# A GNN kernel on one core: layer 0's own terms and head in three fp32r products, and the splits, tiles and window widths rearranged around them

## The chip, the core and the metric

The kernel runs on one core of a Trainium2 chip. The time is the device time of one execution in microseconds (us); lower is better. The engines are named as in the profile: PE is TensorE, DVE VectorE, ACT ScalarE, POOL GpSimd, SP SyncE. Each runs its own list of instructions in order; they meet only through semaphores.

## What is computed

625 nodes with 256 features, 10625 edges (`src`, `dst`, sorted by `dst`, self loops included), float32 throughout:

```python
def _edge_conv(x, src, dst, W, b):
    m = jnp.concatenate([x[dst], x[src] - x[dst]], axis=-1) @ W + b
    s = segment_sum(m, dst, 625);  cnt = segment_sum(ones, dst, 625)
    return s / jnp.maximum(cnt, 1.0)[:, None]

h = relu(layernorm(x)); xs = [h]
for W, b in ((W0, b0), (W1, b1), (W2, b2)):
    h = relu(_edge_conv(h, src, dst, W, b)); xs.append(h)
x = x + concatenate(xs, axis=-1) @ Wf + bf
h = relu(layernorm(x)) @ W                      # second block
agg = segment_sum(edge_weight[:, None] * h[src], dst, 625) + bias
out = x + relu(batchnorm(agg) * gamma + beta)
```

## The kernel before

**Reformulation.** With W split into its upper rows Wa (for `x[dst]`) and lower rows Wb (for `x[src]`), a layer is z / count + own: z is the count matrix (how often node s sends to node d) times u = h Wb, and own = h (Wa - Wb) + b, masked to nodes with an edge. The kernel builds the 625 x 625 count matrix, and a weighted one for the last block, once, then multiplies by it in each layer.

**Building the matrices.** Edges lie in 85 tiles of 125. For a tile `t`, `source_tile(t)` makes a one-hot of the sources (`src_hot`, 125 x 626, bf16): one DVE instruction, or two ACT instructions for the tiles in `SCALAR_TILES` (0, 4, 9, 36, 40, 55, 72, 76). The ring `src_hot` has 36 slots, so tile t waits until the tile 36 before it has been used. As the edges are sorted, the targets of a tile lie in a window of at most 28 nodes; `half_width(t)` gives the half of the range that is multiplied (6 to 14). `plain_window` and `weighted_window` make the target one-hots of 17 tiles at a time on DVE. PE multiplies, for each of five blocks of targets (r) and five of sources (s), all tiles that touch r (19 or 21 "pieces") into one bank of PSUM (L1215). In r = 0 it goes tile by tile; in r = 1 and 2 it goes through the first half of the pieces for all s, and then the second. ACT copies each finished block (`copy_block(r, s)`), and PE may start block (r + 1, s) only then.

**Interleaved with that.** PE's list goes: r = 0 with the transposes of h0 at the pieces named in `jobs` and the small vectors at piece 13; `neighbour_terms_0` (u of layer 0, fp32); r = 1; `own_terms_0` (fp32, eight products of 312 columns); r = 2; r = 3; r = 4; `sums_0` (z, in two halves of columns); `head_0` (h0 times the first 256 rows of Wf, fp32, ten products of 256 columns); then, for layers 1 and 2, `neighbour_terms`, `own_terms`, transposes of the weighted matrix, `sums`, `head`. The later layers don't multiply in fp32: an operand is split into a high part (ACT, a copy to fp32r) and a low part (DVE or POOL, operand minus high part), and `three` makes three fp32r products of them.

DVE's list is one loop over the 85 tiles, in which other work is put at fixed tiles: `U_AT` are the low parts of u in layer 0 (each waits for ACT's high part), `DIFF_AT` is Wa - Wb of layer 0, in place in `raw[0]`, `VECS_AT`, `DEV_AT` and `FLAG_AT` are small. After the loop follows a tail: `difference(1)`, `low_part(HI_WB1)`, `inverse_rows(0)`, `low_part(HI_WD1)`, `inverse_rows(1)`, `edge_rows_of(0)` and `(1)`, `difference(2)`; then the `z_step` and `h_low` of layer 0 and five `add_head(0, b)`, which release PSUM banks. POOL waits for `w_lo_vector` 1 (the tail's first low part), sums the weighted parts of r = 0 and 1, makes a low part, and masks the own terms of layer 0 (`mask_own_0`), for which the first `z_step` waits.

`Groups.plan` gives each group of products a bank of PSUM; `fill(name)` makes PE wait until the group that last used the bank has been read. For layer 1 the groups `("u", 1, b)` go to banks 5, 2, 3, 4, 6, and `("head", 0, b)` to banks 4, 6, 7, 0, 1: so `("u", 1, 3)` waits for `x1_added` 1, the first `add_head`, and `("u", 1, 4)` for the second.

## Time and profile before

| what | value |
|---|---|
| time, three runs | 121.03, 121.14, 122.48 us; median 121.14 |
| the profiled execution: its time | 121.92 us |
| the profiled execution: its span | 120.0 us (all times below count from its start) |
| granted TensorE clock, mean over the span | 0.978 of full speed |
| PE busy (matmuls) | 105.3 us, 88% |
| DVE busy | 96.7 us, 81% |
| ACT busy | 60.9 us, 51% |
| POOL busy | 27.3 us, 23% |
| DMA | 4.63 MB, nearly all of it before 12 us |

A row of a timeline gives the start, the busy time of the run of like instructions, the engine, the line, what is written and read with shapes, how many there are (x), and in brackets how long the engine had been idle and who released it. Durations of neighbours on an engine overlap a little, so a cost is best read from start to start.

### The profile page before, as it was taken

How to read it: one execution, taken by the hardware profiler on the slowest of the kernel's cores; microseconds unless marked ns; L12 is line 12 of the kernel's file. 1: busy time of each engine (PE TensorE's matmuls, PEld its weight loads, DVE VectorE, ACT ScalarE, POOL GpSimd, SP SyncE). 2: the span in 40 equal slices, each digit the busy share in tenths (PEclk: the TensorE clock that was granted, in tenths of full speed). 3: DMA queues.
4: the chain of work that ended last, by engine and by line, in shares of the span. 5: the costliest groups of instructions: out<-in, count | busy, mean ns of one | idle time of the engine just before them, and what ended most of it. 6: DMA issues, size and time to landing. Idle time of an engine off the chain costs nothing.

```text
span 120.0 us, 2668 instructions
## 1 busy us (share of the span) xinstructions
PE 105.3 (88%) x1023; PEld 97.5 (81%) x1023; DVE 96.7 (81%) x275; ACT 60.9 (51%) x143; POOL 27.3 (23%) x32
## 2 busy tenths in 40 slices
PE   0388999989999999999699999999899989999740
PEld 0236898968798999998599999999799979998540
DVE  2499995999999999989996579865999979527860
ACT  2596787986679999131560333331513154232530
POOL 7100000000000039964139910199000000000000
PEclk9999999999999999999999999999999999999965
DMA  1979500000020000500001100000000000000044
GB/s 45 227 194 267 182 2 5 0 5 0 3 87 5 0 5 5 177 8 0 0 0 45 48 0 0 0 5 0 0 0 5 0 0 0 3 0 5 0 102 112
DMA packets 5401, 4.63 MB, mean 39 GB/s; under 512 B 555, under 2 KB 5386, under 8 KB 5386
## 3 DMA queue, kind: packets, MB, share of 16 engines
q1 hardware_dynamic: 4460, 3.68, 10.9%
q10 hardware_dynamic: 926, 0.75, 2.4%
q8 instruction: 10, 0.16, 0.6%
q14 instruction: 5, 0.04, 0.1%
HBM read 3.79 MB, written 0.64 MB: 37 GB/s over the span
## 4 chain that ended last, share of the span: by engine, by line
PE 47%; DVE 38%; issue 6%; ACT 3%; DMA 2%; DVEq 0%; SPq 0%; ACTq 0%
DVE src_hot L567 14%; PE bank L1066 9%; PE bank L1068 9%; PE bank L1310 9%; PE bank L1067 9%; PE bank L1215 4%; DVE inv_count L643 3%; DMA edge_rows_i<-in_dst_dram 2%; DVE stats L517 2%; DVE raw L574 2%; PE bank L1350 2%; PE bank L1128 2%; DVE pre L729 2%; DVE pre L733 2%; DVE h_lo L739 1%
## 5 line engine op out<-in xcount | busy, mean ns | idle before, releaser
L1215 PE MATMUL bank<-dst_hot,src_hot 125*128 125x112 bf16 (+10 forms) x505 | 27.5, 213 | 1.6 <-DVE src_hot L567 1.0
L1215 PEld LDWEIGHTS bank<-dst_hot,src_hot 125*128 125x128 bf16 x505 | 25.1, 103 | 4.6 <-DVE src_hot L567 3.1
L567 DVE TENSOR_SCALAR src_hot<-node_id,edge_cols 125x626 bf16<-125x626 f16 x77 | 23.9, 377 | 0.0
L461 POOL TENSOR_TENSOR parts<-parts 125x625 f32<-125x625 f32 x5 | 7.0, 1394 | 48.7 <-DVE wb_lo L630 40.5
L1310 PE MATMUL bank<-counts,u_lo 125*128 125x312 f32 (+1 forms) x60 | 16.3, 308 | 0.0
L1010 ACT ACTIVATE h_hi<-pre 128x312 fp32r<-128x312 f32 (+1 forms) x12 | 5.6, 466 | 16.5 <-DVE pre L733 16.5
L1310 PE MATMUL bank<-counts,u_hi 125*128 125x312 f32 (+1 forms) x48 | 14.0, 307 | 0.0
L877 ACT ACTIVATE parts<-bank 125x375 f32<-125x375 f32 x25 | 12.9, 535 | 0.0
L1310 PEld LDWEIGHTS bank<-counts,u_lo 125*128 125x128 f32 x60 | 10.9, 189 | 0.0
L1310 PEld LDWEIGHTS bank<-counts,u_hi 125*128 125x128 f32 x48 | 9.1, 189 | 0.0
L877 ACT ACTIVATE counts<-bank 125x125 fp32r<-125x125 f32 (+1 forms) x25 | 7.9, 316 | 1.1 <-PE bank L1215 1.1
L1068 PE MATMUL bank<-wf_lo,h_hi 128*125 128x256 f32 x30 | 8.4, 281 | 0.0
L1066 PE MATMUL bank<-wf_hi,h_hi 128*125 128x256 f32 x30 | 8.4, 281 | 0.0
L1067 PE MATMUL bank<-wf_hi,h_lo 128*125 128x256 f32 x30 | 8.4, 281 | 0.0
L580 DVE TENSOR_TENSOR u_lo<-bank,u_hi 125x256 fp32r<-125x256 f32 (+1 forms) x13 | 5.7, 462 | 2.8 <-ACT u_hi L877 2.6
L877 ACT ACTIVATE u_hi<-bank 125x256 fp32r<-125x256 f32 (+1 forms) x13 | 5.3, 416 | 4.3 <-PE bank L1068 3.4
L877 ACT ACTIVATE weights_hi<-bank 125x500 fp32r<-125x500 f32 (+1 forms) x7 | 3.4, 546 | 7.6 <-PE bank L1350 7.6
L729 DVE TENSOR_TENSOR pre<-bank,inv_count 128x312 f32<-128x312 f32 (+1 forms) x12 | 5.7, 476 | 1.6 <-PE bank L1310 1.6
L733 DVE TENSOR_TENSOR pre<-pre,own 128x312 f32<-128x312 f32 (+1 forms) x12 | 6.3, 521 | 0.9 <-POOL own L472 0.5
L739 DVE SCALAR_TENSOR_TENSOR h_lo<-pre,h_hi 128x312 fp32r<-128x312 f32 (+1 forms) x12 | 6.3, 535 | 0.7
L1066 PE MATMUL bank<-weights_hi,u_hi 125*128 125x312 f32 (+1 forms) x20 | 6.2, 312 | 0.7 <-DVE u_lo L796 0.7
L905 ACT ACTIVATE distance<-node_id,edge_cols 125x626 f16<-125x626 f16 x8 | 6.6, 830 | 0.4 <-DVE edge_cols L551 0.2
(137 smaller groups left out, 260.4 us busy)
## 6 DMA issues: line engine op xcount, KB each, us to landing
raw<-in_L_gnn_W_dram SPq DMA_DIRECT2D x3, 512.0 KB, 6.7
x_in<-in_x_dram ACTq DMA_DIRECT2D x1, 560.0 KB
raw<-in_L_gnn_Wf_dram SPq DMA_DIRECT2D x1, 512.0 KB, 4.0
wf<-in_L_gnn_Wf_dram SPq DMA_DIRECT2D x1, 256.0 KB, 7.7
raw<-in_L_gnn_Wf_dram SPq DMA_DIRECT2D x1, 256.0 KB, 2.8
raw<-in_L_gnn_W_dram SPq DMA_DIRECT2D x1, 256.0 KB, 2.8
out_dram<-x_in SPq DMA_DIRECT2D x1, 224.0 KB
out_dram<-x_in SPq DMA_DIRECT2D x1, 168.0 KB
```

Of the source, the lines that this page charges most:

```text
L461: step.add(pool.tensor_tensor(part[:, :, 1, :], part[:, :, 1, :], part[:, :, 2, :], ALU.add))
L567: dve.tensor_scalar(src_hot[:, t % RING, 0:IDS], node_id[:, 0:IDS], edge_cols[:, 0, t:t + 1], None, ALU.is_equal).then_inc(src_hot_vector, 1)
L729: dve.tensor_tensor(pre_t[:, f, a:e], groups.bank[("z", l, q)][:, 0:e - a], inv_count[:, a:e], ALU.mult).then_inc(z_read, 1)
L733: dve.tensor_tensor(pre_t[:, f, a:e], pre_t[:, f, a:e], own[:, f, a:e], ALU.add).then_inc(z_ready, 1)
L739: dve.scalar_tensor_tensor(out=h_lo[l + 1][:, f, a:e], in0=pre_t[:, f, a:e], scalar=0.0, in1=h_hi[l + 1][:, f, a:e].bitcast(F32), op0=ALU.max,
L877: copy = lambda o, i: nc.scalar.activation(o, i, ACT.Copy)
L905: nc.scalar.activation(distance[:, :], node_id[:, 0:IDS], ACT.Abs, bias=edge_cols[:, 0, t:t + 1], scale=-1.0).then_inc(distance_ready, 1)
L1066: pe.matmul(o, lh, rh, start=start, stop=False)
L1067: pe.matmul(o, ll, rh, start=False, stop=False)
L1068: return pe.matmul(o, lh, rl, start=False, stop=stop)
L1215: return pe.matmul(built[s][:, :, n0:n0 + n], src_hot[:, t % RING, BLK * s:BLK * s + P], dst_hot[:, c, :, j // 2, c0:c0 + n, j % 2], start ...
L1310: ins = pe.matmul(bank[KF * h + f][:, 0:e - a], u[:, k, P * f:P * (f + 1)], counts[0:BLK, k, a:e], start=False, stop=(k == NB - 1 and u is ...
```

## The change

What it does, by place:

- `half_width` has two values, 10 and 14, where it had five (6 to 14). The number of pieces stays 101; the columns per block of sources go from 8256 to 8832.
- h0 is transposed at pieces 9, 11, 12, 14 and 15 (before: 12, 12, 14, 14, 16); ACT copies a transposed block after the next normalised one, not two later.
- Tile 36 goes from ACT to DVE.
- DVE's loop: `difference(0)` at tile 28 (before 37); the low parts of u at 34, 39 and 42 (27, 32, 35); new are the low part of Wa - Wb of layer 0 at 44 and the low parts of h0 at 46 and 48.
- ACT: new are three copies after r = 0 (the high part of Wa - Wb, two of h0) and one after r = 2 (the high part of Wf's first rows).
- `own_terms_0` and `head_0` use `three` on the split operands. `own_terms_0` waits for the new low parts.
- DVE's tail: the low part of Wf's first rows comes in, `low_part(HI_WD1)` and `difference(2)` go behind layer 0's last `h_low`, ahead of `add_head`. With that ACT's high part of layer 2's Wa - Wb goes behind layer 0's h, and `wf23_hi` into layer 1.
- POOL starts on `w_diff` 2, i.e. after `difference(1)`.

```diff
-SCALAR_EARLY, SCALAR_LATER = (0, 4, 9), {0: (36, 40), 1: (55,), 2: (72, 76)}
+SCALAR_EARLY, SCALAR_LATER = (0, 4, 9), {0: (40,), 1: (55,), 2: (72, 76)}
-STATS_AT, SHIFT_AT, VECS_AT, DIFF_AT = (1, 2, 3, 5, 6), 8, 19, 37
-U_AT = (27, 32, 35)
+STATS_AT, SHIFT_AT, VECS_AT, DIFF_AT = (1, 2, 3, 5, 6), 8, 19, 28
+WD0_AT, H0_AT = 44, (46, 48)
+U_AT = (34, 39, 42)
-    return min(WINDOW // 2, 2 * round(2.5 + 9 * math.sqrt(p * (1 - p))))
+    return 10 if 5 + 18 * math.sqrt(p * (1 - p)) < 10.75 else WINDOW // 2
+        h0_hi = sb("h0_hi", [P, KF, NODES_E], F32R)
+        (h0_lo,) = overlay(h0_base, arena_top[0], [("h0_lo", [P, KF, NODES_E], F32R)])
+        wd[0], (wf0_hi, wf0_lo) = wd[2], w4
-            pool.wait_ge(w_lo_vector, 1)
+            pool.wait_ge(w_diff, 2)
+                if t == WD0_AT:
+                    dve.wait_ge(layer0_hi, 1)
+                    dve.tensor_tensor(wd[0][1][:, :, :], raw[0][:, 0:KF, :], wd[0][0][:, :, :].bitcast(F32),
+                                      ALU.subtract).then_inc(layer0_lo, 1)
+                if t in H0_AT:
+                    f = H0_AT.index(t)
+                    dve.wait_ge(h0_hi_ready, f + 1)
+                    dve.tensor_tensor(h0_lo[:, f, :], h0_t[:, f, :], h0_hi[:, f, :].bitcast(F32),
+                                      ALU.subtract).then_inc(h0_lo_ready, 1)
             difference(1)
-            low_part(HI_WB1, wb[1][1][:, :, :], raw[1][:, KF:2 * KF, :], wb[1][0][:, :, :])
...
             inverse_rows(0)
-            low_part(HI_WD1, wd[1][1][:, :, :], raw[1][:, 0:KF, :], wd[1][0][:, :, :])
+            dve.wait_ge(layer0_hi, 2)
+            dve.tensor_tensor(wf0_lo[:, :, :], wf0[:, :, :], wf0_hi[:, :, :].bitcast(F32),
+                              ALU.subtract).then_inc(layer0_lo, 1)
+            low_part(HI_WB1, wb[1][1][:, :, :], raw[1][:, KF:2 * KF, :], wb[1][0][:, :, :])
...
-            difference(2)
...
                 h_low(l, 3)
+                if l == 0:
+                    low_part(HI_WD1, wd[1][1][:, :, :], raw[1][:, 0:KF, :], wd[1][0][:, :, :])
+                    difference(2)
                 if l < LAYERS - 1:
                     for b in range(NB):
                         add_head(l, b)
...
+                if r == 0:
+                    act.wait_ge(w_diff, 1)
+                    copy(wd[0][0][:, :, :], raw[0][:, 0:KF, :]).then_inc(layer0_hi, 1)
+                    for f in range(KF):
+                        copy(h0_hi[:, f, :], h0_t[:, f, :]).then_inc(h0_hi_ready, 1)
+                if r == 2:
+                    act.wait_ge(wf0_loaded, 16)
+                    copy(wf0_hi[:, :, :], wf0[:, :, :]).then_inc(layer0_hi, 1)
...
-                pe.wait_ge(w_diff, 1)
+                pe.wait_ge(layer0_lo, 1)
+                pe.wait_ge(h0_lo_ready, KF)
...
-                        ins = pe.matmul(o, raw[0][:, k, P * f:P * (f + 1)], h0_t[:, k, a:e],
-                                        start=(k == 0), stop=(k == KF - 1))
+                        ins = three(o, (wd[0][0][:, k, fc], wd[0][1][:, k, fc]), (h0_hi[:, k, a:e], h0_lo[:, k, a:e]),
+                                    k == 0, k == KF - 1)
...
-            jobs = {12: (0, 1), 14: (2, 3), 16: (4,)}
+            jobs = {9: (0,), 11: (1,), 12: (2,), 14: (3,), 15: (4,)}
```

## Rows read from the trace of the kernel before

**Rows 1.** Timeline of DVE, loop over tiles: start us, busy us, engine line op.

```profile
16.28 2.43 DVE L567 TENSOR_SCALAR src_hot<-node_id,edge_cols 125x626 bf16<-125x626 f16 x8
20.18 0.69 DVE L580 TENSOR_TENSOR u_lo<-bank,u_hi 125x512 fp32r<-125x512 f32 x1 [1.47 <-ACT u_hi L877]
...
29.91 0.41 DVE L556 TENSOR_TENSOR dst_hot<-pair_id,rel 125x504 bf16<-125x504 f16 x1
...
31.22 4.78 DVE L567 TENSOR_SCALAR src_hot<-node_id,edge_cols 125x626 bf16<-125x626 f16 x16
...
37.23 2.14 DVE L567 TENSOR_SCALAR src_hot<-node_id,edge_cols 125x626 bf16<-125x626 f16 x7
...
39.65 3.00 DVE L567 TENSOR_SCALAR src_hot<-node_id,edge_cols 125x626 bf16<-125x626 f16 x10
```

**Rows 2.** Timeline of PE: r = 1 to 4, own terms and head of layer 0.

```profile
21.81 3.57 PE L1215 MATMUL bank<-dst_hot,src_hot 125*128 125x4 bf16 x60
25.80 2.20 PE L1215 MATMUL bank<-dst_hot,src_hot 125*128 125x12 bf16 x45 [0.43 <-DVE src_hot L567]
27.86 4.46 PE L1139 MATMUL bank<-h_t,raw 128*128 128x312 f32 x16
32.16 2.40 PE L1215 MATMUL bank<-dst_hot,src_hot 125*128 125x12 bf16 x50
...
37.23 8.44 PE L1215 MATMUL bank<-dst_hot,src_hot 125*128 125x12 bf16 x181
...
52.70 4.48 PE L1149 MATMUL bank<-wf,h_t 128*125 128x256 f32 x20
```

**Rows 3.** Timeline of PE: neighbour terms, then own terms of layer 1.

```profile
59.87 0.38 PE L1066 MATMUL bank<-wb_hi,h_hi 128*125 128x256 f32 x1 [1.19 <-DVE h_lo L739]
...
60.67 0.28 PE L1066 MATMUL bank<-wb_hi,h_hi 128*125 128x256 f32 x1
...
62.10 0.31 PE L1066 MATMUL bank<-h_hi,wd_hi 128*128 128x312 f32 x1
...
65.59 1.03 PE L1350 MATMUL bank<-ident,parts 125*125 125x125 f32 x8
```

**Rows 4.** Timeline of ACT, after the copies of r = 2.

```profile
37.79 0.91 ACT L905 ACTIVATE distance<-node_id,edge_cols 125x626 f16<-125x626 f16 x1
...
41.03 0.61 ACT L877 ACTIVATE wb_hi<-raw 128x512 fp32r<-128x512 f32 x1
41.55 0.25 ACT L877 ACTIVATE counts<-bank 125x125 fp32r<-125x125 f32 x1
```

**Rows 5.** Timeline of DVE: the tail, and layer 0's first and last steps.

```profile
42.58 0.67 DVE L574 TENSOR_TENSOR raw<-raw 128x512 f32<-128x512 f32 x1
43.18 0.67 DVE L630 TENSOR_TENSOR wb_lo<-raw,wb_hi 128x512 fp32r<-128x512 f32 x1
...
45.84 1.32 DVE L630 TENSOR_TENSOR wd_lo<-raw,wd_hi 128x512 fp32r<-128x512 f32 x1
...
49.75 1.76 DVE L574 TENSOR_TENSOR raw<-raw 128x512 f32<-128x512 f32 x1
...
52.39 0.89 DVE L733 TENSOR_TENSOR pre<-pre,own 128x312 f32<-128x312 f32 x1 [0.49 <-POOL own L472]
...
59.73 0.41 DVE L656 TENSOR_TENSOR x_in<-x_in,bank 125x256 f32<-125x256 f32 x1
```

**Rows 6.** Timeline of POOL: first sum of weights, own terms masked.

```profile
43.93 1.30 POOL L461 TENSOR_TENSOR parts<-parts 125x625 f32<-125x625 f32 x1 [40.54 <-DVE wb_lo L630]
...
50.92 2.01 POOL L472 TENSOR_TENSOR own<-own,has_edge 128x312 f32<-128x312 f32 x2
```

**Rows 7.** Timeline of PE, the end of the kernel.

```profile
112.98 1.00 PE L1394 MATMUL bank<-ident,pre 128*125 128x128 f32 x5 [0.82 <-ACT pre L1052]
115.00 1.26 PE L1394 MATMUL bank<-ident,pre 128*125 128x128 f32 x4 [1.01 <-ACT pre L1052]
```

**Rows 8.** Busy time by stretch: start:end, length, PE busy, granted clock, DMA share, GB/s.

```profile
115.00:116.00 1.00, 1.00 (x4) 0.50 0.21 53
```

More of the change, by code:

```diff
@@ L223, in gnn_kernel @@
         shift = sb("shift", [P, NB], F32)
+        h0_base = arena_top[0]
         h0_t = sb("h0_t", [P, KF, NODES_E], F32)
@@ L316, in gnn_kernel @@
         h0_t_ready = sem("h0_t_ready")
+        h0_hi_ready = sem("h0_hi_ready")
+        h0_lo_ready = sem("h0_lo_ready")
+        layer0_hi = sem("layer0_hi")
+        layer0_lo = sem("layer0_lo")
         w_diff = sem("w_diff")
@@ L400, in gnn_kernel @@
                     (raw[2], rows(W4), raw_loaded[2], (w_lo_pool, 3))]
-        LO_W = (None, (w_lo_vector, 2), (w_lo_pool, 3))
+        LO_WB = (None, (w_lo_vector, 1), (w_lo_pool, 2))
+        LO_WD = (None, (w_lo_vector, 2), (w_lo_pool, 3))
         LO_WF1, LO_WF23, LO_W4 = [(w_lo_pool, n) for n in (1, 4, 5)]
@@ L942, in _ @@
                                      scale=rstd[0:BLK, b:b + 1]).then_inc(h0_ready, 1)
-                if b >= 2:
-                    h0_high(b - 2)
-            h0_high(3)
-            h0_high(4)
+                if b >= 1:
+                    h0_high(b - 1)
+            h0_high(NB - 1)
             def copy_block(r, s):
@@ L980, in _ @@
             high_part(wb[2][0][:, :, :], raw[2][:, KF:2 * KF, :])
-            act.wait_ge(w_diff, 3)
-            high_part(wd[2][0][:, :, :], raw[2][:, 0:KF, :])
             def turned(i):
@@ L1006, in _ @@
                         turned_high(i)
+                if l == 1:
+                    act.wait_ge(raw_loaded[1], 32)
+                    high_part(wf23_hi[:, :, :], raw[1][:, :, :])
                 for q, (f, h) in enumerate(QUADS):
@@ L1011, in _ @@
                 if l == 0:
-                    act.wait_ge(raw_loaded[1], 32)
-                    high_part(wf23_hi[:, :, :], raw[1][:, :, :])
+                    act.wait_ge(w_diff, 3)
+                    high_part(wd[2][0][:, :, :], raw[2][:, 0:KF, :])
                 if l == 1:
@@ L1137, in own_terms_0 @@
                     o = fill(("own", 0, q))[:, 0:e - a]
+                    fc = slice(P * f, P * (f + 1))
                     for k in range(KF):
-                        ins = pe.matmul(o, raw[0][:, k, P * f:P * (f + 1)], h0_t[:, k, a:e],
-                                        start=(k == 0), stop=(k == KF - 1))
+                        ins = three(o, (wd[0][0][:, k, fc], wd[0][1][:, k, fc]), (h0_hi[:, k, a:e], h0_lo[:, k, a:e]),
+                                    k == 0, k == KF - 1)
                     ins.then_inc(filled, 1)
             def head_0():
-                pe.wait_ge(wf0_loaded, 16)
+                pe.wait_ge(layer0_lo, 2)
                 for b in range(NB):
-                    o = fill(("head", 0, b))[0:BLK, 0:D]
-                    for k in range(KF):
-                        ins = pe.matmul(o, h0_t[:, k, BLK * b:BLK * (b + 1)], wf0[:, k, :],
-                                        start=(k == 0), stop=(k == KF - 1))
-                    ins.then_inc(filled, 1)
+                    project(("head", 0, b), feature_rows(h0_hi, h0_lo, b),
+                            [(wf0_hi[:, k, :], wf0_lo[:, k, :]) for k in range(KF)])
             def neighbour_terms(l):
@@ L1221, in _ @@
                     for i in range(len(pieces)):
+                        if i == 12:
+                            turn_vecs()
                         for b in jobs.get(i, ()):
                             turn_h0(b)
-                        if i == 13:
-                            turn_vecs()
                         wait_tile(seen)
@@ L1355, in _ @@
             for l in range(1, LAYERS):
-                pe.wait_ge(*LO_W[l])
+                pe.wait_ge(*LO_WB[l])
                 neighbour_terms(l)
+                pe.wait_ge(*LO_WD[l])
                 own_terms(l)
```

## The prediction

> **What bounds the kernel now.** I read the page's busy shares and chain first: PE and DVE are both busy most of the time, and the chain that ends last changes between them. So the question is which of the two ends last in each stage, and for that I went through the timelines of PE, DVE, ACT and POOL side by side.
>
> To 42.6 us the tiles of DVE lead. A tile costs 0.293 us (ten from 39.65 to 42.58), the two window instructions of 17 tiles 1.31 us (29.91 to 31.22). The loop has one real hole: tiles 19 to 26 begin at 16.28 and end at 16.28 + 8 x 0.293 = 18.62, and the next instruction, a low part of u, begins at 20.18 because ACT's high part is late [rows 1]. PE runs just behind: it waits for a tile at 25.80 in r = 1, does the own terms from 27.86 to 32.16 (4.3 us), r = 2 with two small jobs to 37.23 (5.07 us), r = 3 and 4 to 46.58, where it hardly waits [rows 2]. From 42.58 DVE's tail lasts to 51.9, and the first `z_step` then waits for POOL's mask until 52.39 [rows 5, 6]. DVE's steps of layer 0 lead on to 59.73, and PE, which had been idle for 1.19 us, goes on at 59.87. After that it is PE that leads through layers 1 and 2: the neighbour terms' last three blocks take 59.87 to 62.10, the own terms of layer 1 62.10 to 65.59, with no hole [rows 3]. So before 37 us what counts is when DVE's tiles and PE's r = 2 are done, from there to 59.8 POOL's start and DVE's steps, and after 59.87 each hole in PE.
>
> **The change, part by part.**
>
> *PE's own savings.* Own terms of layer 0: 4.30 us now [rows 2]. In three fp32r products they are the same 24 products as layer 1's, 3.49 us [rows 3]: 0.8 us less. Head: 52.70 to 57.04, 4.34 us; 30 products of 256 columns at the pace of 18 in 2.23 us (59.87 to 62.10) take 3.7 us: 0.6 us less. The head lies ahead of PE's 1.19 us of idle, which waits for DVE [rows 3], so its gain is worth nothing; the own terms' gain counts only if they can start in time.
>
> *DVE's loop up to tile 48.* Added are tile 36 (0.29), the low part of Wa - Wb (an operation like the one from 42.58 to 43.18, 0.60 us [rows 5]) and two low parts of h0. These have 626 columns instead of 512: 0.07 fixed and 0.53 x 626/512 make 0.72 each. Sum 2.33 us. `difference(0)` and the low parts of u only move. With the low parts of u at tile 34 and later, ACT's high parts (ready at 20.1) are long there, so the hole of 20.18 - 18.62 = 1.56 us goes. Net +0.8 us. The windows before tile 49 stood at 29.91 [rows 1] and come at 30.7; the second low part of h0 lies one tile ahead of them and is done at 30.4.
>
> *What waits for it.* `own_terms_0` now waits for both low parts of h0, i.e. until 30.45. When is PE there? Tile 35 comes at 18.62 + 8 tiles (2.34) + `difference(0)` 0.60 + windows 1.31 + low part 0.6 = 23.5 and is ready at 23.9, before PE's second half of r = 1, so the wait at 25.80 [rows 2] goes and r = 1 takes about 4.9 us from 21.8: ready at 26.7. Two widths and earlier transposes change r = 0 by at most 0.4 us either way (four of its 19 pieces go from 96 to 112 columns, and the last h0 transposes need `vecs`, which DVE makes at tile 19, as now); I take PE at 26.7 to 27.1. PE stands for 3.4 us or more, where it stood 0. The own terms run 30.45 to 33.95, and r = 2 begins 1.8 us later than at 32.16. Nothing can be put into this hole: r = 2 is behind the own terms in PE's list.
>
> *To the end of the tiles.* r = 2 ends at 33.95 + 5.07 = 39.0, its last block at 38.9. DVE reaches tile 68, which needs that block's slots, at 37.23 + 2 x 0.293 + 0.8 = 38.6 [rows 1], waits 0.3 and ends the tiles 1.1 us late, at 43.7. On ACT the copies of r = 2 end 1.8 us later than at 37.79; then there is a new copy of 512 columns (0.52, as from 41.03 to 41.55), tiles 72 and 76 (37.79 to 41.03, 3.24) and `wb_hi` 0.52. The first copy of r = 3 thus begins at 43.9 instead of 41.55 [rows 4], and PE's r = 4 waits for it until 44.45, where r = 3 ends at 44.1. Afterwards PE is 2.0 us late: z's first half, 46.58 to 49.5 now, is filled at 51.6.
>
> *The widths.* 576 more columns for each of 5 sources are 2880; at the pace of r = 2 that would be 1.2 us. But r = 3 and 4, with narrow pieces in them, take no less per piece (181 from 37.23 in 8.44 us, 47 ns with waits) than the first half of r = 2 (50 in 2.40 us, 48 ns with 112 columns [rows 2]). I take 0, the ends are -0.2 and +0.5.
>
> *Tail and POOL.* Out of the tail go a low part (1.3 us beside POOL) and `difference(2)` (1.7), in comes one low part of 0.6 to 1.3, and `wb_lo`, 0.6 now, may take 1.3 beside POOL [rows 5]. The tail of 8.9 us becomes 6.5 to 7.9, and DVE is ready for `z_step` at 51.6 at the latest. But it isn't DVE that opened it: POOL's mask did, seven us of work after its start at 43.93 [rows 6]. POOL now starts after `difference(1)`, one low part (0.6) sooner after the tiles: 43.93 + 1.1 - 0.6. So the first `z_step` is 0.5 us late, about 52.9, and z at 51.6 is just in time. Layer 0's steps keep their length: DVE is through with them at 60.3 instead of 59.73.
>
> *The moved work.* There now stand `low_part(HI_WD1)` and `difference(2)`, 0.60 each with POOL idle, ahead of the first `add_head` (0.41). PE starts its last three blocks of neighbour terms at 60.4, is ready for `("u", 1, 3)` 0.8 later (59.87 to 60.67 [rows 3]), at 61.2, and must wait for that `add_head`: 60.3 + 1.2 + 0.45 = 61.95. It was at 60.67: 1.3 us late in a stage where PE leads and had no hole. On ACT the high part for layer 2 waits for `difference(2)` until 61.5 and the high parts of u queue behind it; they are needed at 63 to 66, which leaves room. Wf's rows for the later heads are loaded from 61 instead of 47; needed past 67, so they are hidden.
>
> Sum at unchanged clock: +1.3 us (0.5 from POOL's start, 0.8 from the bank wait; the 1.8 to 2.0 us of PE are inside, absorbed but for that).
>
> *The clock.* PE would stand 3.4 us with nothing to do. The one fall of the clock in this trace comes after less: idle 0.82 us, five transposes, idle 1.01 us, and in 115 to 116 the granted clock is 0.50, the 1.2 GHz level [rows 7, 8]. An idle of 1.19 us did no harm: at 62.10 to 65.59 a product of 312 columns takes 0.145 us [rows 3]. 3.4 us is far beyond both, so the fall is likelier than not. A product of 312 columns takes 0.26 us at 1.2 GHz. The cost lies between 0 (no fall) and 24 x 0.115 = 2.8 us (all own terms low); I take nine products, 1.0 us, since it can fall only shortly before the 24 start and their dense work should bring it back. All of it arrives, because the sum above has used up PE's room.
>
> The Trainium skill speaks against the change here: "TensorE: Matmul & The Clock Gate", Part 1, has half clock as the state without work, released by activity, and its table at the end warns against idle gaps between bursts. By that rule the time is the one with 1.0 us in it, without it 1.0 us less.
>
> Total: +1.3 + 1.0 = +2.3. The sum is made in an execution with span 120.0 and time 121.92. Its start-to-start steps are the same in the others, so I put the difference on the median: 121.14 + 2.3 = **123.5**.
>
> **Rivals.**
>
> *The clock holds.* 121.14 + 1.3 = 122.5. For it: after the idle of 1.19 us nothing fell. Against: the hole is three times as long.
>
> *The delay is absorbed, no change.* PE and DVE lose at r = 2, but the tail is 2.3 us lighter. If POOL's path from 43.93 to 52.2 shrinks (its five operations of 1.30 alone are 6.5 of 7.0 us) by its 0.5 and DVE's low parts of h0 cost 0.6, layer 0 ends as now, and only the bank wait of 0.8 or less stays: 121.1 to 121.9, in the middle 121.5. Against: it needs each step to come out at its low end.
>
> *Faster.* The single mechanism is POOL's start: it follows the end of the tiles 0.6 us sooner, and POOL opens `z_step`. It decides if the low parts of h0 were ready when PE comes to them, so that the tiles end at 43.4 or sooner, and if PE's wait for the bank is hidden by the head's 0.6 us. That gives up to 0.6 + 0.5 less: 120.0. Against it: 30.4 against 26.7 to 27.1 is no close race.
>
> *The change's gain doesn't exist at all* (three products as slow as fp32): worth 0.8 us more in the own terms, 124.3; rows 3 show 3.49 us for that very shape, so I give it nothing of its own.
>
> **How the numbers follow.** Clock falls: 0.42, with 122.8 to 125.3 about 123.5, skewed upward, since the term's bound lies 1.8 above what I took. Clock holds: 0.33, 121.9 to 123.3. Absorbed: 0.15. Faster: 0.07. The rest, 0.03, is a clock that stays low into r = 2, above 125.3. The range of 8 in 10 leaves out the faster case with a little of the absorbed one, and the top: 121.2 to 125.0. A change by 2% is 2.4 us, about what can be told here: slower begins at 123.56. A little over half of the first case, a bit of the second and the rest are above: 0.36. Faster by over 2% (below 118.7) needs more than any mechanism above gives: 0.04. Within: 0.60.
>
> **What would show it.** Right: the second low part of h0 ends near 30.4 and PE's first own product is released by it, with 3 us or more of idle ahead; a granted clock below 1 between 27 and 36; tiles end near 43.7; the first mask of POOL opens `z_step` near 53; PE's eighteen products after layer 0 have a hole of about 0.7 us before `("u", 1, 3)`, released by `x_in`. Wrong: own terms that start at 27 to 28; tiles that end by 42.6; a `z_step` that starts near 51.5; or PE with no hole at 61.

## The result, and the profile after

| | before | after |
|---|---|---|
| time, us (median, lowest to highest) | 121.4 (121.03 to 122.48) | 124.92 (123.52 to 125.89) |
| ratio to before, 95% interval | 1 | 1.0237, [1.0172, 1.0301] |
| the profiled execution, us | 121.92 | 125.05 |
| its span, us | 120.0 | 123.2 |

The change costs 3.5 us by the medians, 2.9 us by the ratio, and 3.1 us by the two profiled executions, whose steps can be compared one by one. The ratio leaves out the slowest of after's four executions (125.89 us, mean granted clock 0.950), which counts as slow. The loss is clear of the noise; the interval does not decide whether it is more or less than 2%. I forecast 123.5 us in a range of 121.2 to 125.0: the time lies in the range, near its top, and what was forecast as 2.3 us is 2.9 to 3.5.

Busy shares and the clock's row on the page of after (busy us, share of the span, instructions; then the granted clock in 40 slices, 9 being 90% or more of 2.4 GHz):

```profile
span 123.2 us, 2705 instructions
...
PE 105.8 (86%) x1041; PEld 99.6 (81%) x1041; DVE 99.9 (81%) x274; ACT 62.1 (50%) x145; POOL 27.3 (22%) x32
...
PEclk9999999999589999999999999999999999999995
```

PE's clock is down in two places: near slice 10, which is new, and in the last slice, as before. The timeline of PE in after around the new one (start us, busy us, engine, line, operation, count, in brackets the idle time before it and what ended it):

```profile
23.00 4.92 PE L1245 MATMUL bank<-dst_hot,src_hot 125*128 125x12 bf16 x105
...
30.76 0.38 PE L1097 MATMUL bank<-h_hi,wd_hi 128*128 128x312 f32 x1 [2.84 <-issue]
30.98 0.31 PE L1098 MATMUL bank<-h_hi,wd_lo 128*128 128x312 f32 x1
...
32.01 0.46 PE L1097 MATMUL bank<-h_hi,wd_hi 128*128 128x312 f32 x1
...
34.95 0.31 PE L1097 MATMUL bank<-h_hi,wd_hi 128*128 128x314 f32 x1
...
35.82 2.41 PE L1245 MATMUL bank<-dst_hot,src_hot 125*128 125x12 bf16 x50
...
46.44 3.23 PE L1245 MATMUL bank<-dst_hot,src_hot 125*128 125x12 bf16 x76 [0.62 <-ACT parts L900]
```

And busy time by stretch of after (start:end, length, PE busy, granted clock, DMA share, GB/s):

```profile
30.00:31.00 1.00, 0.24 (x2) 1.00 0.00 0
31.00:32.00 1.00, 1.00 (x6) 0.65 0.00 0
32.00:33.00 1.00, 1.00 (x5) 0.50 0.00 0
...
34.00:35.00 1.00, 1.00 (x7) 0.64 0.00 0
35.00:36.00 1.00, 1.00 (x12) 1.00 0.00 0
```

Against [rows 2]: r = 1 has lost its wait for a tile and runs in one piece, but the own terms, which followed it without a gap at 27.86, begin at 30.76 after PE stood 2.84 us. The first products run at the high level; at 31.3 the clock falls to 1.2 GHz and is back at 34.7. The own terms take 5.06 us (30.76 to 35.82), longer than the 4.30 us of the fp32 products that they replace. The trace calls the releaser of the 2.84 us "issue"; the timeline of DVE shows whose end it matches, the second low part of h0, which runs from 29.86 to 30.66. The own terms begin 0.10 us behind it, and 0.09 to 0.11 us behind it in e1_fill, e2_early, e3_heads_first, e4_fp32_head, e7_combo and e11_moved_later too, wherever it lies.

```profile
29.86 0.80 DVE L629 TENSOR_TENSOR h_lo<-h_t,h_hi 128x626 fp32r<-128x626 f32 x1
...
40.88 1.56 DVE L577 TENSOR_SCALAR src_hot<-node_id,edge_cols 125x626 bf16<-125x626 f16 x5 [2.03 <-PE bank L1245]
...
45.64 0.67 DVE L584 TENSOR_TENSOR raw<-raw 128x512 f32<-128x512 f32 x1
...
48.31 1.33 DVE L683 TENSOR_TENSOR w_lo<-wf,w_hi 128x512 fp32r<-128x512 f32 x1
49.55 1.78 DVE L649 TENSOR_TENSOR wb_lo<-raw,wb_hi 128x512 fp32r<-128x512 f32 x1
...
53.33 0.67 DVE L667 TENSOR_SCALAR has_edge<-bank 128x250 f32<-128x250 f32 x2
53.92 0.47 DVE L749 TENSOR_TENSOR pre<-bank,inv_count 128x312 f32<-128x312 f32 x1
55.04 0.93 DVE L753 TENSOR_TENSOR pre<-pre,own 128x312 f32<-128x312 f32 x1 [0.65 <-POOL own L482]
```

DVE, which had passed the same place without a stop [rows 1], waits 2.03 us for r = 2's last block, and its tiles end at 45.64 instead of 42.58 [rows 5]. The two rows of POOL in after that answer to [rows 6]:

```profile
46.40 1.30 POOL L471 TENSOR_TENSOR parts<-parts 125x625 f32<-125x625 f32 x1 [42.99 <-ACT parts L900]
...
54.08 1.55 POOL L482 TENSOR_TENSOR own<-own,has_edge 128x312 f32<-128x312 f32 x2 [0.34 <-DVE has_edge L667]
```

The first row names ACT's copies as the releaser, but POOL starts 0.09 us after `difference(1)` has ended (45.64 + 0.67 = 46.31). It is 0.08 or 0.09 us in e4_fp32_head, e6_tail, e7_combo and e10_pool_start as well, so it is DVE that releases it, and the ACT copy that is named only ended at nearly the same time.

Last, PE in the neighbour terms of layer 1, against [rows 3]:

```profile
62.60 0.38 PE L1097 MATMUL bank<-wb_hi,h_hi 128*125 128x256 f32 x1 [0.54 <-DVE h_lo L759]
...
64.13 0.39 PE L1097 MATMUL bank<-wb_hi,h_hi 128*125 128x256 f32 x1 [0.57 <-DVE x_in L675]
```

Where the 3.1 us come from, by landmarks of the stages (us from the span's start, read off the timelines):

| landmark | before | after | difference |
|---|---|---|---|
| r = 0 done on PE, next stage begins | 17.41 | 18.61 | +1.20 |
| own terms of layer 0 begin | 27.86 | 30.76 | +2.90 |
| r = 2 begins | 32.16 | 35.82 | +3.66 |
| DVE's tiles end | 42.58 | 45.64 | +3.06 |
| first `z_step`: its addition | 52.39 | 55.04 | +2.65 |
| layer 0's last low part ends | 59.81 | 62.54 | +2.73 |
| own terms of layer 1 begin | 62.10 | 65.65 | +3.55 |
| the second output half's transposes | 115.00 | 118.51 | +3.51 |
| end of the span | 120.03 | 123.17 | +3.14 |

The loss is made by 35.82, 0.6 us of it is gone again by the end of the tiles, the tail gives 0.4 us back, and the moved work takes 0.8 us. From there the two run in step for 53 us. Before loses its clock at 114.81 and after at 120.05, which gives back 0.4 us at the end.

### The profile page after: what moved, and what is told of

It reads as the page before. It is cut to its first block, busy times and chain, and to the rows that moved or that the text cites. A ratio compares the mean times of both kernels' runs of the same rounds, so it can differ in the third digit from the quotient of the medians.

```text
span 123.2 us, 2705 instructions
## 1 busy us (share of the span) xinstructions
PE 105.8 (86%) x1041; PEld 99.6 (81%) x1041; DVE 99.9 (81%) x274; ACT 62.1 (50%) x145; POOL 27.3 (22%) x32
## 4 chain that ended last, share of the span: by engine, by line
PE 44%; DVE 28%; ACT 8%; issue 7%; POOL 7%; DMA 3%; SPq 0%; POOLq 0%; DVEq 0%; ACTq 0%
PE bank L1097 10%; PE bank L1099 10%; DVE src_hot L577 10%; PE bank L1098 10%; PE bank L1340 8%; DMA edge_rows_i<-in_dst_dram 3%; POOL parts L471 2%; POOL parts L473 2%; PE bank L1245 2%; DVE stats L527 2%; ACT parts L900 2%; PE bank L1380 2%; DVE pre L753 2%; DVE h_lo L759 1%; ACT distance L928 1%
## 5 line engine op out<-in xcount | busy, mean ns | idle before, releaser
L1245 PE MATMUL bank<-dst_hot,src_hot 125*128 125x112 bf16 (+6 forms) x505 | 27.6, 215 | 1.3 <-ACT parts L900 0.6
L1245 PEld LDWEIGHTS bank<-dst_hot,src_hot 125*128 125x128 bf16 x505 | 25.6, 104 | 3.8 <-DVE src_hot L577 1.8
L577 DVE TENSOR_SCALAR src_hot<-node_id,edge_cols 125x626 bf16<-125x626 f16 x78 | 24.7, 380 | 2.0 <-PE bank L1245 2.0
L471 POOL TENSOR_TENSOR parts<-parts 125x625 f32<-125x625 f32 x5 | 7.0, 1392 | 50.2 <-ACT parts L900 43.0
L1097 PE MATMUL bank<-h_hi,wd_hi 128*128 128x312 f32 (+1 forms) x24 | 8.2, 342 | 2.8 <-issue 2.8
L1098 PE MATMUL bank<-h_hi,wd_lo 128*128 128x312 f32 (+1 forms) x24 | 8.0, 335 | 0.0
L1099 PE MATMUL bank<-h_lo,wd_hi 128*128 128x312 f32 (+1 forms) x24 | 8.0, 333 | 0.0
L753 DVE TENSOR_TENSOR pre<-pre,own 128x312 f32<-128x312 f32 (+1 forms) x12 | 6.9, 573 | 1.0 <-POOL own L482 0.6
L1097 PEld LDWEIGHTS bank<-h_hi,wd_hi 128*128 128x128 f32 x24 | 5.1, 212 | 2.9 <-issue 2.9
L473 POOL TENSOR_TENSOR parts<-parts 125x625 f32<-125x625 f32 x5 | 6.8, 1369 | 0.4
```

What stands on the lines that cost most here:

```text
L471: step.add(pool.tensor_tensor(part[:, :, 1, :], part[:, :, 1, :], part[:, :, 2, :], ALU.add))
L473: pool.tensor_tensor(part[:, :, 0, :], part[:, :, 0, :], part[:, :, 1, :], ALU.add).then_inc(weights_summed, 1)
L577: dve.tensor_scalar(src_hot[:, t % RING, 0:IDS], node_id[:, 0:IDS], edge_cols[:, 0, t:t + 1], None, ALU.is_equal).then_inc(src_hot_vector, 1)
L753: dve.tensor_tensor(pre_t[:, f, a:e], pre_t[:, f, a:e], own[:, f, a:e], ALU.add).then_inc(z_ready, 1)
L1097: pe.matmul(o, lh, rh, start=start, stop=False)
L1098: pe.matmul(o, ll, rh, start=False, stop=False)
```

## The experiments

The four parts of the theory are: (1) the own terms wait for the low parts of h0, (2) this hole drops the clock, (3) the tail ends by POOL's and DVE's sums together, (4) the moved work opens a hole in layer 1. The rivals were that it is enough to fill the hole, that the cost sits in the head or in the widths, and that POOL's earlier start is a gain. All times are medians; "its own before" is the kernel before, run beside it on the same chip.

### e1_fill: the hole filled with products

```
                o = fill(("own", 0, 0))
                for _ in range(13):
                    pe.matmul(o[:, :], zeros_bf[:, :], node_id[:, 0:512], start=True, stop=True)
                pe.wait_ge(layer0_lo, 1)
```

The 13 added products write zeros into a bank that the own terms then start anew: they are extra work that changes no result.

> The changed kernel, with 13 products of zeros (512 columns, bf16) into the bank of the first own term, put on PE between r = 1 and the waits of own_terms_0; they fill 2.8 us of the hole and change no result. Theory (the clock costs 1.6 us, since the own terms took 5.06 us instead of 3.49): the own terms still start near 30.8 us, released by DVE, the granted clock stays 1.00 from 27 to 37 us, they take 3.5 us, and the whole is 1.3 to 1.6 us shorter than the changed kernel: 123.4 against 124.9. Rival (the clock is a bystander and the time is set by DVE, ACT and POOL after it): r = 2 begins 1.6 us sooner but the end moves by less than 0.4 us.

Measured: 123.65 us, 1.0139 [1.006, 1.0219] to its own before (121.93). PE in e1_fill:

```profile
27.49 2.97 PE L1167 MATMUL bank<-node_id,zeros_bf 125*128 125x512 f16 x13
...
31.12 0.39 PE L1097 MATMUL bank<-h_hi,wd_hi 128*128 128x312 f32 x1 [0.66 <-issue]
...
34.68 1.52 PE L1248 MATMUL bank<-dst_hot,src_hot 125*128 125x12 bf16 x30
```

and its stretches, in the same columns as above:

```profile
31.00:32.00 1.00, 0.88 (x6) 1.00 0.00 0
32.00:33.00 1.00, 1.00 (x9) 1.00 0.00 0
```

The own terms still wait, to 31.12, but they run at the high level and take 3.56 us instead of 5.06. r = 2 begins 1.14 us sooner than in after, the tiles end 1.14 us sooner (44.50), the span is 1.3 us shorter. By the ratios it is 1.2 us (1.0237 to 1.0139), but the two intervals overlap, so the times alone would not show it. The clock's fall is worth about 1.15 to 1.3 us, less than the 1.5 us by which the own terms got shorter, because they began 0.36 us later here.

That the fall comes from PE standing does not rest on this run alone. All four profiled executions with a hole of 2.7 to 3.0 us ahead of the own terms (after, e3_heads_first, e4_fp32_head, e11_moved_later) have a fall between 30.5 and 31.3 us and take 5.06 or 5.07 us for the own terms. All four in which the hole is filled, short or absent (e1_fill, e2_early, e9_early_fill, e7_combo) have none there and take 3.55 or 3.56 us. The profiled execution of e1_fill has another fall, from 13.53 to 16.94 us, ahead of the edit; r = 0 still ends 0.29 us sooner in it than in after.

### e2_early: the same low parts, up to seven tiles sooner

```
-WD0_AT, H0_AT = 44, (46, 48)
-U_AT = (34, 39, 42)
+WD0_AT, H0_AT = 38, (39, 40)
+U_AT = (34, 36, 37)
```

> The changed kernel, with the same splits at earlier tiles: low parts of u at 34, 36, 37, low part of Wa - Wb at 38, low parts of h0 at 39 and 40. DVE does the same work up to tile 48. Theory (PE's hole costs twice, as standing and through the clock): second low part of h0 done near 28.2 us instead of 30.7, hole of PE under 1 us, clock 1.00, r = 2 begins near 31.8 instead of 35.8; DVE then doesn't wait for r = 2 and its tiles end near 43.5 instead of 45.6; the whole is 2 us shorter, 122.9. Rival 1 (only the clock matters): 1.5 us shorter, as much as with the filling products. Rival 2 (DVE's added work sets the end of the tiles, not PE): tiles end near 45 and the gain is under 0.7 us.

Measured: 123.33 us, 1.0116 [1.0029, 1.0203], 1.6 us less than after by the medians where 2 were forecast. PE and DVE in e2_early:

```profile
28.15 0.39 PE L1097 MATMUL bank<-h_hi,wd_hi 128*128 128x312 f32 x1 [1.43 <-issue]
...
31.71 1.46 PE L1245 MATMUL bank<-dst_hot,src_hot 125*128 125x12 bf16 x29
...
43.40 0.67 DVE L584 TENSOR_TENSOR raw<-raw 128x512 f32<-128x512 f32 x1
```

The own terms now take 3.56 us without a fall of the clock, r = 2 begins 0.45 us ahead of before, and the tiles end 2.24 us sooner than in after. Layer 0 ends 2.26 us sooner (60.28). But the span is only 0.9 us shorter in this execution. Of that 2.26 us, 1.4 are lost again in layer 1, where two waits (times: us in total, how many, longest) and a fall of the clock stand:

```profile
PE bank L1097 <- DVE h_lo L759: 1.2, 1, 1.2
...
PE bank L1097 <- DVE x_in L675: 0.6, 1, 0.6
```

```profile
61.00:62.00 1.00, 0.44 (x4) 1.00 0.09 6
62.00:63.00 1.00, 1.00 (x7) 0.70 0.32 81
63.00:64.00 1.00, 1.00 (x7) 0.50 1.07 380
```

PE, sooner through z and the head, waits longer for layer 0, then again for `x_in`, and at 62.4 it falls to 1.2 GHz until 65.8. The other three executions have spans of 120.9, 120.7 and 121.9 us. So a hole mended in one place had moved to the next.

### e9_early_fill: e2_early with five zero products ahead of layer 1's third block

```
+                    if l == 1 and b == 2:
+                        o = fill(("u", l, b))
+                        for _ in range(5):
+                            pe.matmul(o[:, :], zeros_bf[:, :], node_id[:, 0:512], start=True, stop=True)
```

Here too the added products change no result.

> The kernel with the splits at earlier tiles (38, 39, 40), and in layer 1 five products of zeros ahead of the third block of neighbour terms, in the 1.2 us in which PE waits for DVE; they go into that block's own bank and change no result. Theory (in the run with the early splits the clock fell at 62.4 us, after holes of 1.18 and 0.56 us, and took 1.7 us back): the clock stays at 1.00 from 20 to 110 us, the end is 1.3 to 1.7 us earlier than with the early splits alone, near 121.0 of span or less. Rival (the fall there was chance, or the time isn't set by PE in layer 1): within 0.5 us of the run with early splits.

Measured: 123.30 us, 1.0119 [1.007, 1.0168], no faster than e2_early. In e9_early_fill's profiled execution the fall at 62.4 is gone, and the last output half begins at 116.27, 1.47 us sooner than in e2_early (117.74). The span is nevertheless 122.1, because SyncE's four issues of the last output transfers take 3.48 us, where they took 2.19 in e2_early:

```profile
59.01 1.25 PE L1189 MATMUL bank<-node_id,zeros_bf 125*128 125x512 f16 x5
...
116.10 3.48 SPq L437 DMA_DIRECT2D out_dram<-x_in  x4
```

One of the four took 1.87 us; the others take 0.37 to 0.49. The mean spans are 121.5 for e9_early_fill and 121.45 for e2_early. The forecast gain of 1.3 to 1.7 us did not come, and the rival named above it stands: the fall in e2_early may have been one execution's. A possible reading of the equal medians is that most executions of e2_early had no fall there. Neither that, nor that the products removed it in e9_early_fill, nor that it costs e2_early's median anything, is shown.

### e3_heads_first: the moved work behind the third `add_head`

```
-                if l == 0:
-                    low_part(HI_WD1, wd[1][1][:, :, :], raw[1][:, 0:KF, :], wd[1][0][:, :, :])
-                    difference(2)
                 if l < LAYERS - 1:
                     for b in range(NB):
+                        if l == 0 and b == 3:
+                            low_part(HI_WD1, wd[1][1][:, :, :], raw[1][:, 0:KF, :], wd[1][0][:, :, :])
+                            difference(2)
                         add_head(l, b)
```

> The changed kernel, with low_part(HI_WD1) and difference(2) behind the third add_head of layer 0 instead of ahead of the first. Theory (the moved work keeps PE waiting for a bank): the hole of 0.57 us before u of block 3 is gone, nothing else moves, 0.5 to 0.6 us shorter than the changed kernel. Rival (the wait is made up later, as DVE's work for layer 1 comes late anyway, or the moved work now makes own_terms of layer 1 or ACT's high parts late): less than 0.2 us, with a new hole between 63 and 68 us.

Measured: 125.48 us, with spans from 121.7 to 124.4: the times vary too much to say that it gained or lost. The trace says more. The wait of 0.57 us for `x_in` is gone: from layer 0's last low part (62.30) to layer 1's own terms (64.59) it takes 2.29 us, as before (59.81 to 62.10), against 3.11 in after. But `difference(2)` stands now ahead of the low parts of u, and PE waits for one of those. PE in e3_heads_first:

```profile
65.95 0.41 PE L1097 MATMUL bank<-h_hi,wd_hi 128*128 128x312 f32 x1 [0.33 <-DVE u_lo L590]
...
68.78 1.03 PE L1380 MATMUL bank<-ident,parts 125*125 125x125 f32 x8
```

The own terms of layer 1 take 4.19 us (64.59 to 68.78) instead of 3.49 [rows 3]: 0.8 us won, 0.7 lost. The wait was moved, not removed, as the rival had it.

### e11_moved_later: the two pieces apart

```
                         low_rows(("u", l, b), b, NB * l + b + 1)
+                    if l == 1:
+                        difference(2)
...
                     for b in range(NB):
+                        if l == 0 and b == 3:
+                            low_part(HI_WD1, wd[1][1][:, :, :], raw[1][:, 0:KF, :], wd[1][0][:, :, :])
                         add_head(l, b)
```

ACT's high part of layer 2's Wa - Wb, which needs `difference(2)`, goes into layer 1 with it.

> The changed kernel, with the low part of layer 1's Wa - Wb behind the third add_head and difference(2) behind the five low parts of u of layer 1 (the run that kept both together behind the third add_head got rid of one wait for a bank and got another, 0.33 us and slow products after it). Theory: with difference(2) out of the way the low parts of u come in time, PE has no hole from the third block on, own terms of layer 1 take 3.5 us and begin 0.8 us sooner after layer 0's last low part; spans 0.8 us shorter than the changed kernel's at a like clock. Rival (the stage is set by something else): no more than 0.2 us.

Measured: 123.73 us, 1.0107 [1.0031, 1.0182]. PE in e11_moved_later:

```profile
62.18 0.38 PE L1097 MATMUL bank<-wb_hi,h_hi 128*125 128x256 f32 x1 [0.55 <-DVE h_lo L759]
...
64.41 0.31 PE L1097 MATMUL bank<-h_hi,wd_hi 128*128 128x312 f32 x1
```

The stage is at 2.29 us again (62.12 to 64.41), and no new wait appears in the own terms behind it, which take 3.49 us (64.41 to 67.90). The gain is 1.2 us by the medians and 1.6 by the ratios, whose intervals just overlap. Only 0.8 of that is this stage by the traces. Another part is the start: r = 0 ends 0.30 us sooner in this execution than in after, the own terms of layer 0 begin 0.41 us sooner, and that lies ahead of the edit in the program, so the edit did not make it.

### e4_fp32_head: the head in fp32 again

```
-                pe.wait_ge(layer0_lo, 2)
+                pe.wait_ge(wf0_loaded, 16)
                 for b in range(NB):
-                    project(("head", 0, b), feature_rows(h0_hi, h0_lo, b),
-                            [(wf0_hi[:, k, :], wf0_lo[:, k, :]) for k in range(KF)])
+                    o = fill(("head", 0, b))[0:BLK, 0:D]
+                    for k in range(KF):
+                        ins = pe.matmul(o, h0_t[:, k, BLK * b:BLK * (b + 1)], wf0[:, k, :],
+                                        start=(k == 0), stop=(k == KF - 1))
+                    ins.then_inc(filled, 1)
```

With it go the high and the low part of Wf's first rows; the low part of h0 has memory of its own.

> The changed kernel, with the head of layer 0 in fp32 again: no high and low part of Wf's first rows (0.52 us on ACT after r = 2, 1.24 us in DVE's tail), low parts of h0 in memory of their own, since the head reads h0. Theory (the head's own gain lies in PE's idle, its splits lie on the path through ACT's tiles 72 and 76, and DVE's tail): head 0.7 us longer and unnoticed, r = 4 begins 0.5 us sooner, the first z_step 0.5 to 1.0 us sooner; the whole 0.5 to 1.0 us shorter. Rival (head's gain counts, the splits are hidden): up to 0.7 us longer.

Measured: 123.86 us, 1.0091 [1.0039, 1.0144] to its own before; 1.1 us less than after by the medians, 1.8 by the ratios, whose intervals do not overlap. DVE in e4_fp32_head:

```profile
48.01 1.32 DVE L648 TENSOR_TENSOR wb_lo<-raw,wb_hi 128x512 fp32r<-128x512 f32 x1
...
52.85 0.48 DVE L745 TENSOR_TENSOR pre<-bank,inv_count 128x312 f32<-128x312 f32 x1 [0.85 <-PE bank L1336]
...
54.05 0.93 DVE L749 TENSOR_TENSOR pre<-pre,own 128x312 f32<-128x312 f32 x1 [0.72 <-POOL own L481]
```

From the end of the tiles (45.34) to the first multiplication of `z_step` it is 7.5 us instead of 8.3, and there the block of z is what it waits for. The addition comes 8.7 us after the tiles instead of 9.4. PE's wait for ACT's copies ahead of r = 4 (0.62 us at 46.44 in after) is gone as well. Nothing later pays for the slower products. The three-product head is a loss by itself: it shortens PE where PE waits [rows 3] and lengthens DVE where DVE leads.

### e5_widths: before with the two widths

```
-    return min(WINDOW // 2, 2 * round(2.5 + 9 * math.sqrt(p * (1 - p))))
+    return 10 if 5 + 18 * math.sqrt(p * (1 - p)) < 10.75 else WINDOW // 2
```

> The kernel before with the two widths alone (half ranges of 10 and 14 instead of 6 to 14; 2880 more columns in all). Theory (pieces of 96 columns take 55 ns, those of 112 take 51, those of 64 as long as those of 80, so the width costs nothing on PE): r = 4 takes 4.0 us and the end of the span is within 0.3 us of before's. Rival (columns cost what the clock says, 0.42 ns each): r = 0 and r = 4 are 0.4 us longer each, the whole 0.4 to 0.8 us longer.

Measured: 122.02 us against 121.72, 1.0027 [0.9992, 1.0062]: no difference that can be told, and at most 0.75 us. PE in e5_widths, r = 3 and 4:

```profile
36.80 8.41 PE L1215 MATMUL bank<-dst_hot,src_hot 125*128 125x12 bf16 x181
```

The same 181 pieces took 8.44 us before [rows 2]: wider pieces at the edges cost nothing here.

### e10_pool_start: before with POOL's start alone moved

```
-            pool.wait_ge(w_lo_vector, 1)
+            pool.wait_ge(w_diff, 2)
```

> The kernel before, with POOL's start alone changed (after difference(1) instead of after the low part behind it). Theory of the prediction (POOL's mask opens the first z_step, and its start counts in full): z_step's add 0.6 us sooner, layer 0's last low part 0.6 us sooner, the whole 0.6 us shorter; the run with the lighter tail then owes the other 0.6 us of its 1.2 to fewer operations of DVE beside POOL's. Rival (DVE's tail is what opens it: the step can't start before the tail ends at 51.4 us with its add at 51.9): 0.5 us at z_step at most, and the whole at most 0.4 us shorter.

Measured: 121.29 us against 121.33, 0.999 [0.9953, 1.0028]. POOL, then DVE in e10_pool_start:

```profile
43.64 1.69 POOL L461 TENSOR_TENSOR parts<-parts 125x625 f32<-125x625 f32 x1 [40.24 <-ACT parts L877]
```

```profile
52.52 0.83 DVE L733 TENSOR_TENSOR pre<-pre,own 128x312 f32<-128x312 f32 x1 [0.53 <-POOL own L472]
```

POOL starts 0.76 us behind the end of the tiles instead of 1.35 (43.93 - 42.58 [rows 5, 6]), but its first sum now runs beside `wb_lo` and takes 1.69 instead of 1.30. The addition comes 9.64 us after the tiles instead of 9.81. Of 0.6 us, 0.17 arrive there, and nothing that can be told at the end.

### e6_tail: before with a lighter tail

On the kernel before, own terms and head in fp32: POOL's start as in e10_pool_start, and `low_part(HI_WD1)` and `difference(2)` out of the tail, to the places that they have in e11_moved_later:

```
-            low_part(HI_WD1, wd[1][1][:, :, :], raw[1][:, 0:KF, :], wd[1][0][:, :, :])
             inverse_rows(1)
...
             edge_rows_of(1)
-            difference(2)
...
+                    if l == 1:
+                        difference(2)
...
+                        if l == 0 and b == 3:
+                            low_part(HI_WD1, wd[1][1][:, :, :], raw[1][:, 0:KF, :], wd[1][0][:, :, :])
                         add_head(l, b)
```

ACT's high parts for layer 2 and for Wf move with them, and PE waits for the low part of layer 1's Wa - Wb only ahead of the own terms, no longer ahead of the neighbour terms.

> The kernel before, with only its DVE tail and POOL's start changed, and layer 0 left in fp32: POOL starts after difference(1), the low part of layer 1's Wa - Wb goes behind the third add_head, difference(2) behind the five low parts of u of layer 1. Theory (the tail and POOL's start open the first z_step, and the moved work is harmless where PE doesn't wait for it): tiles end as before near 42.6, the first z_step's add starts near 51.8 instead of 52.4, no hole at the third block's bank, and the end is 0.6 us earlier than before. Rival (it only moves the wait: POOL's operations collide with DVE's and take longer, or the low part of Wa - Wb comes late for PE): within 0.2 us of before.

Measured: 120.35 us against 121.72, 0.9888 [0.9854, 0.9922]: faster than both kernels, and by 1.4 us where 0.6 were forecast. DVE, then POOL in e6_tail:

```profile
42.46 0.67 DVE L575 TENSOR_TENSOR raw<-raw 128x512 f32<-128x512 f32 x1
...
49.40 0.48 DVE L728 TENSOR_TENSOR pre<-bank,inv_count 128x312 f32<-128x312 f32 x1 [0.83 <-PE bank L1313]
...
51.08 0.94 DVE L732 TENSOR_TENSOR pre<-pre,own 128x312 f32<-128x312 f32 x1 [1.20 <-POOL own L473]
```

```profile
43.22 1.68 POOL L462 TENSOR_TENSOR parts<-parts 125x625 f32<-125x625 f32 x1 [39.81 <-ACT parts L880]
...
46.24 1.30 POOL L462 TENSOR_TENSOR parts<-parts 125x625 f32<-125x625 f32 x1
...
50.12 1.55 POOL L473 TENSOR_TENSOR own<-own,has_edge 128x312 f32<-128x312 f32 x2
```

POOL's third sum in before, for comparison:

```profile
46.57 1.76 POOL L461 TENSOR_TENSOR parts<-parts 125x625 f32<-125x625 f32 x1
```

The addition comes 8.62 us after the tiles instead of 9.81: 1.2 us, of which POOL's start has 0.17 (e10_pool_start). The rest is that DVE no longer runs `wd_lo` and a difference beside POOL: the third sum takes 1.30 us instead of 1.76, the two masks 1.55 instead of 2.01, 0.92 of the 1.0 us. The 1.3 us stay to the end: the own terms of layer 1 start at 60.83 instead of 62.10.

### e7_combo: all mends on the kernel after

The edits of e9_early_fill, e11_moved_later and e4_fp32_head together.

> All mends together: splits at tiles 38, 39, 40; head of layer 0 in fp32 without its splits; low part of layer 1's Wa - Wb behind the third add_head and difference(2) behind the low parts of u of layer 1; five products of zeros in the hole of layer 1. Theory: what is left of the change is own terms in three products, 0.8 us more of DVE work before the tiles end, POOL's earlier start and a lighter tail. Tiles end near 43.4, first z_step's add near 52.0, no fall of the clock before 110 us; span 119.5 to 120.2, i.e. as before or 0.4 us less. Rival (own terms in three products are worth their splits): over 1 us less than before.

Measured: 122.04 us against 121.72, 1.0033 [1.0008, 1.0059]. PE in e7_combo:

```profile
28.20 0.38 PE L1090 MATMUL bank<-h_hi,wd_hi 128*128 128x312 f32 x1 [0.36 <-issue]
```

r = 2 begins at 31.75, 0.4 us ahead of before, and still DVE's tiles end at 43.45 instead of 42.58, for the low parts of Wa - Wb and h0, and tile 36, are on DVE. The first addition is at 52.13 where e6_tail has it at 51.08. So the own terms in three products buy nothing even when they hardly wait. The 1.7 us between e6_tail and e7_combo are not theirs alone, though: widths, transposes, tile 36 and the zero products differ too.

## Why the prediction was right, and where it was off

- **The own terms wait for the low parts of h0.** Right: forecast to end near 30.4, measured 30.66; forecast idle 3.4 us or more, measured 2.84. The hole was shorter since r = 0 ended 1.2 us later, which I had put at 0.4 us at most: the trace's record of the clock begins with a rise at 17.65 instead of 15.83 (the views show 1.00 before it, but two transposes take 0.63 us at 16.77 and 0.39 at 17.66), so that more pieces of 112 columns and transposes ran at the low level. It did no harm, as PE had to wait anyway. This was chance, not the change: e2_early and e9_early_fill have the same instructions up to layer 1, and their first rise is at 14.61 and 18.07, the end of r = 0 at 17.41 and 18.74.
- **The clock falls.** Right, and the term was mis-sized: 1.0 us by nine slow products, measured 1.57 (5.06 - 3.49), by 13 products in 3.4 us. The step "it can fall only shortly before the 24 start" failed: it fell after the hole, 0.5 us into the own terms. e1_fill gives 1.15 to 1.3 us of it back at the end. By the Trainium skill, "TensorE: Matmul & The Clock Gate", Part 1, half clock is what PE has without work; the trace agrees that a hole brings it, but it came when PE was at work again.
- **The tiles.** DVE's wait for r = 2's block was forecast at 0.3 us, 1.3 with the clock, and is 2.03; the tiles end at 45.64, forecast 43.7 and 44.7 with the clock. The missing 0.9 us are the 0.6 of the clock and 0.3 by which the own terms began later. z's first half, forecast filled at 51.6 or 52.6 with the clock, has its last product start at 53.66; DVE took it at 53.92 without a recorded wait, so this added nothing. PE's wait for ACT's copies ahead of r = 4, forecast 0.35, is 0.62 at 46.44.
- **The tail.** Mis-sized: 6.5 to 7.9 us forecast, 8.3 measured (45.64 to 53.92). The one low part "of 0.6 to 1.3" is 1.24, and `wb_lo` is 1.71, for which I had allowed 1.3. Both run beside POOL.
- **POOL opens `z_step`.** Half right. The row at 55.04 has POOL as its releaser, as forecast, and the addition is 0.4 us sooner after the tiles than before, where I had 0.6. But POOL had itself waited 0.34 us for DVE's `has_edge`. e10_pool_start shows the step "one low part (0.6) sooner" to be wrong as a gain: POOL's start alone gives 0.17. What gives time is the work taken away from beside POOL (e6_tail). In after `wb_lo` and the new low part took its place.
- **The bank wait in layer 1.** Right: forecast about 0.7 us of hole released by `x_in`, measured 0.57 at 64.13, and the stage is 0.82 us longer. e11_moved_later removes it, 3.11 to 2.29 us.
- **Widths at 0, head's gain at 0.** Right (e5_widths, within its interval; e4_fp32_head). Of the head I had only seen that it gains nothing; that its splits cost 0.7 us at the first addition, and about 1 us or more in all, I had inside the tail and not named.
- **The sum.** 0.5 + 0.8 + 1.0 = 2.3 forecast. By the traces, at the same places: 2.65 at the first addition (forecast 1.5 with the clock), 0.8 to 0.9 in layer 1 and -0.4 at the end, 3.1. The miss of 0.8 us by the traces (0.6 to 1.2 by the times) comes from ahead of the first addition: clock 0.6, start of the own terms 0.3, tail 0.2, less the 0.4 at the end. So the mechanisms were as forecast and the term of the clock was the one sized worst.
- **The rivals.** The clock did not hold; e1_fill, which keeps it up, comes to 1.0139, near that rival's 122.5 over 121.14, a ratio of 1.011. The delay was not absorbed. The faster case needed the low parts of h0 by 26.7 to 27.1; in e2_early, which comes nearest at 28.1, the layer still ends 0.5 us later than before.

What stays open: how often e2_early loses its clock in layer 1 (one profiled execution shows it), and where the rest of the difference between after and e11_moved_later comes from. The price of the clock also differs between executions of after: their mean clocks of 0.973, 0.984, 0.977 and 0.950 make 6.5, 3.9, 5.7 and 12.4 us at the low level (twice the missing share of the span), and only the first was profiled. The move of tile 36 and the earlier transposes were not tried alone. Whether the own terms would pay with the low parts of h0 made by ACT or POOL was not tried.

## What to carry to other kernels

Before products are made cheaper by splitting their operands, ask which engine makes the parts and when: here 0.8 us on PE were bought with 2.0 us of low parts on DVE (0.60 + 2 x 0.72), which led, and the parts came 2.8 us after the products could have run. A hole in a busy PE is priced twice, as the wait and as the clock behind it, so the work that precedes it must be ready first or the split not made. Where two engines both use the same memory, look for operations to take out of the overlap before moving a start: the start gave 0.17 us, the lighter overlap 1.0.

## What the runs showed of the hardware

- The clock fell at 31.3 us, 0.5 us after a hole of 2.84 us had ended, and was back at 34.7. Holes of 2.95, 3.03 and 2.72 us did the same in e3_heads_first, e4_fp32_head and e11_moved_later, with the fall 0.1 to 0.8 us behind the hole's end. With the hole filled it stayed up (e1_fill). In e2_early two short holes, 1.18 and 0.56 us with work between them, were followed by a fall (62.4 to 65.8), although 1.19 us alone did nothing in before [rows 3] and 1.43 us alone nothing at 28.15 in the same kernel.
- A DVE operation with two operands in SBUF and 512 elements takes 0.60 us by itself and 1.0 to 1.7 beside POOL; POOL's sums take 1.30 and beside it 1.63 to 1.76 (rows of before, after, e10_pool_start, e6_tail). Which one pays differs: `wd_lo` and the third sum in before are both longer (1.24 and 1.76), while in e10_pool_start and e6_tail `wb_lo`, which starts 0.16 us ahead of POOL's first sum, keeps its 0.60 and the sum alone takes 1.69 or 1.68. The Trainium skill, "SBUF — State Buffer", "Who interferes with whom", says that a DVE instruction with two SBUF inputs contends with a GpSimd one that reads SBUF; the traces agree.
- One issue of an output transfer on SyncE took 1.87 us instead of 0.33 to 0.49 (e9_early_fill, at 117.21 us). No run explains it.
